# The row maxima of windowed attention, taken off in 16 products of 64 rows instead of 8 of 128

## The reference

```python
def local_attention(q, k, v):              # 8 heads of 64, window of 64 tokens
    ...
    bk, bv = (look_around(bk), look_around(bv))   # each window sees itself and the one before
    sim = jnp.einsum('bhwid,bhwjd->bhwij', bq, bk)
    mask = (i < j) | (i > j + WINDOW) | (j == -1)
    sim = jnp.where(mask, -jnp.finfo(sim.dtype).max, sim)
    attn = jax.nn.softmax(sim, axis=-1)
    out = jnp.einsum('bhwij,bhwjd->bhwid', attn, bv)
```

## Time and profile before

| | us |
|---|---|
| median of 3 runs | 1603.91 |
| the runs | 1602.45, 1603.91, 2719.34 |
| the profiled execution | 1603.7 |
| its span in the trace | 1601.9 |

### The profile page before, as it was taken

The page is one execution under the profiler, slowest core; times in us unless marked ns, Lnnn a source line. Parts: engine busy times, 40 slices in busy tenths (PEclk is TensorE's granted clock), DMA queues, the critical chain, the costliest instruction groups (busy, mean ns, idle before and its releaser), DMA issues.

```text
span 1601.9 us, 46856 instructions
## 1 busy us (share of the span) xinstructions
PE 1433.1 (89%) x19077; PEld 1139.4 (71%) x19077; DVE 1266.0 (79%) x1704; ACT 1288.6 (80%) x1970; POOL 1124.4 (70%) x690
## 2 busy tenths in 40 slices
PE   5999987889999999999997567889999999999998
PEld 3777865677777777777776454777777777777776
DVE  6777757878888888888875867878888888888874
ACT  4876867788888888888886757688888888888885
POOL 3332206778888888888873545778888888888872
PEclk9999999999999999999999879999999999999999
DMA  4312004676666556665650003675666557565662
GB/s 117 103 43 89 20 11 80 129 121 121 114 124 118 115 123 122 118 115 117 119 100 8 1 7 77 128 120 117 120 122 117 117 119 124 123 119 115 117 103 63
DMA packets 359858, 157.50 MB, mean 98 GB/s; under 512 B 299410, under 2 KB 335836, under 8 KB 359644
## 3 DMA queue, kind: packets, MB, share of 16 engines
q1 hardware_dynamic: 359644, 154.51, 48.7%
HBM read 27.29 MB, written 6.29 MB: 21 GB/s over the span
## 4 chain that ended last, share of the span: by engine, by line
PE 36%; ACT 24%; DVE 16%; POOL 9%; issue 8%; DMA 6%; SPq 1%; DVEq 0%; POOLq 0%; ACTq 0%
PE PS L200 6%; PE PS L202 5%; PE PS L201 5%; DMA t<-t 5%; POOL t L1498 5%; POOL t L1504 3%; DVE t L1319 3%; ACT t L1104 3%; ACT t L1125 3%; ACT t L1179 2%; ACT t L1091 2%; PE PS L883 2%; PE PS L902 2%; DVE t L1348 2%; PE PS L858 2%
## 5 line engine op out<-in xcount | busy, mean ns | idle before, releaser
L1498 POOL TENSOR_TENSOR t<-t 128x1024 f32<-128x1024 f32 x128 | 439.7, 3435 | 167.1 <-DVE t L1319 133.7
L1504 POOL TENSOR_TENSOR t<-t 128x512 f32<-128x512 f32 x256 | 320.7, 1274 | 18.4
L1313 DVE TENSOR_REDUCE t<-t 128x16 f32<-128x1024 f32 x128 | 156.0, 1219 | 93.7 <-ACT t L1091 93.7
L200 PE MATMUL PS<-wqh,HH 128*128 128x512 f32 x384 | 170.4, 444 | 33.8 <-DVE t L1319 19.8
L1091 ACT ACTIVATE t<-PS 128x1024 f32<-128x1024 f32 x128 | 131.4, 1026 | 62.3 <-PE PS L202 62.3
L1319 DVE SCALAR_TENSOR_TENSOR t<-t,PS 128x1024 f32<-128x1024 f32 x128 | 155.2, 1213 | 20.1 <-ACT t L1098 20.1
L883 PE MATMUL PS<-t 128*64 128x65 f32 x4096 | 147.5, 224 | 24.3 <-DVE t L1382 22.6
L1348 DVE TENSOR_REDUCE t<-PS 128x8 bf16<-128x1024 f32 x128 | 156.1, 1219 | 15.7 <-PE PS L832 15.5
L1104 ACT CAST t<-t 128x1024 bf16<-128x1024 f32 x128 | 133.2, 1041 | 36.5 <-POOL t L1504 34.3
L1329 DVE TENSOR_TENSOR t<-t 128x1024 f32<-128x1024 f32 x128 | 156.9, 1226 | 4.4
L1336 DVE TENSOR_TENSOR t<-t,PS 128x1024 bf16<-128x1024 f32 x128 | 155.4, 1214 | 6.2 <-ACT PS L1111 6.2
(11 more groups left out here) (252 smaller groups left out, 3597.1 us busy)
## 6 DMA issues: line engine op xcount, KB each, us to landing
t<-t SPq DMA_DIRECT2D x254, 130.0 KB, 2.4
t<-turns SPq DMA_DIRECT2D x128, 128.0 KB, 2.6
t<-yT SPq DMA_DIRECT2D x108, 128.0 KB
t<-t SPq DMA_TRANSPOSE x304, 3.2
t<-in_c_rope SPq DMA_DIRECT2D x32, 128.0 KB, 2.1
turns<-t SPq DMA_DIRECT2D x32, 128.0 KB, 1.9
t<-in_L_attn_a_x SPq DMA_DIRECT2D x4, 512.0 KB, 7.0
t<-yT SPq DMA_DIRECT2D x16, 127.8 KB
```

What stands on the lines that cost most here:

```text
L200: e.matmul(o, ah, bh, start=not more, stop=False, skip_group_check=True)
L1498: e.e.tensor_tensor(BL.tc.rearrange("p (x h) d -> p x h d", x=2), BL.qn.rearrange("p (x h) d -> p x h d", x=2), sin.to_broadcast([128, 2, ...
L1504: e.e.tensor_tensor(tv[:, :, 32 * s:32 * s + 32], tv[:, :, 32 * s:32 * s + 32], BL.tc[:, :, 32 * (1 - s):32 * (1 - s) + 32], ALU.add).then ...
```

## The change

The eight products of L865 become sixteen of half the rows and half the columns, in the order pair, window, parity: an even head's product reads the maxima and the identity from partitions 0 to 63, an odd head's from 64 to 127. The maxima of window w lie in `rows[w]`, so those of the even heads' second window and the odd heads' first window are in the wrong half. DVE therefore copies 64 by 4 numbers down and 64 by 4 up into columns 8 to 11 of a wider `mx`, behind a wait for its own reduction, and PE waits for the two copies (`la_mo`).

```diff
-                           L=arena(sc, [2, 4, RQ * 128 + 64], BF16), mx=[arena(sc, [8], BF16) for _ in range(2)],
+                           L=arena(sc, [2, 4, RQ * 128 + 64], BF16), mx=[arena(sc, [12], BF16) for _ in range(2)],
...
             def take_off_maxima(i):
-                e.wait_ge(S.la_mr, hi(i) + 1)
-                for s in range(2):
-                    for c in range(4):
-                        mm = e.e.matmul(PS[:, 4 + s, 128 * c:128 * c + 128],
-                                        BL.mx[i % 2][:, 4 * s + c:4 * s + c + 1].to_broadcast([128, 128]), idb[:, :],
-                                        start=False, stop=True, skip_group_check=True)
+
+
+                e.wait_ge(S.la_mo, 2 * hi(i) + 2)
+                for c in range(4):
+                    for w in range(2):
+                        for s in range(2):
+                            at, x = 128 * c + 64 * w, (4 * s if w == s else 8) + c
+                            mm = e.e.matmul(PS[:, 4 + s, at:at + 64], BL.mx[i % 2][rows[s], x:x + 1].to_broadcast([64, 128]),
+                                            idb[rows[s], 64 * s:64 * s + 64], start=False, stop=True, skip_group_check=True)
                 mm.then_inc(S.la_s, 1)
...
-                e.e.tensor_reduce(BL.mx[i % 2], PS[:, 2:4, :].rearrange("p s (c k) -> p (s c) k", k=128), AX.X, ALU.max,
+                mx = BL.mx[i % 2]
+                e.e.tensor_reduce(mx[:, 0:8], PS[:, 2:4, :].rearrange("p s (c k) -> p (s c) k", k=128), AX.X, ALU.max,
                                   negate=True).then_inc(S.la_mr, 1)
+                e.wait_ge(S.la_mr, hi(i) + 1)
+                e.e.tensor_copy(mx[0:64, 8:12], mx[64:128, 0:4]).then_inc(S.la_mo, 1)
+                e.e.tensor_copy(mx[64:128, 8:12], mx[0:64, 4:8]).then_inc(S.la_mo, 1)
```

More of the change, by code:

```diff
@@ L64, in build @@
             "tb_ld tr_ld tr_sc tr_st ys_l sl_hi sl_lo ys_f sf_hi sf_lo "
-            "la_pj la_sq la_ss la_rn la_qn la_ta la_tc la_rp la_hi la_hp la_lo la_ht la_lt la_mx la_mr "
+            "la_pj la_sq la_ss la_rn la_qn la_ta la_tc la_rp la_hi la_hp la_lo la_ht la_lt la_mx la_mr la_mo "
             "la_v la_va la_own la_past la_s la_e la_d la_rc la_ot la_ox la_oe la_po la_out la_k0 "
```

## The result

The changed kernel takes 1739.72 us (median of four runs, 1736.05 to 1742.06), before 1605.28 us in the same comparison (median of four). That is 134 us slower, where I had forecast 18. One of the four runs of before took 2719.34 us; the ratio leaves it out and is 1.083, with a 95% interval from 1.080 to 1.085.

The account below looks back on a forecast made before the run. The chain that ended last, not one engine, was taken to bound the kernel. DVE's 31 x 0.43 = 13.3 us and PE's 4.4 us, about +18, on 1603.7 gave 1622 us; the 8-in-10 range was 1600 to 1633.

Parts of the forecast that it names:

- What bounds the kernel: Layers: no engine alone, but the chain that ended last, crossing the engines in turn, 36.6 us per round of four steps.
- What the products cost: PE, L865 to L891: sixteen products take 0.27 us instead of 0.46, a gain of 0.20 us a tile.
- 44 crossings: Times L865 stands on the chain that ended last, so a PE gain counts at most 44 times, not 128.
- What the copies cost: DVE, between reduction and divide: each copy bounded between 0.066 and 0.19 us, taken as 0.155.
- The first rival: DVE's copies are nearly free and PE's gain goes through: below 1608 us, chance 0.18, half of it below 1600.
- The second rival: DVE's copies cost over twice a plain one, 0.28 us each: slower by over 2%, chance 0.10.
- The wait for the reduction, and no overlap: DVE: waiting for its own reduction costs 0.115 us, and each copy its full 0.155 us without overlap.
- D: Delay of DVE's divide by the wait and the two copies: between 0.25 and 0.50 us, taken as 0.43.
- Who waits for DVE: PE's L891 waits for the divide, moving +0.28 or +0.10 us; the products' wait for the copies is hidden.
- The sum: Over the chain's crossings: DVE 13.3 us and PE 4.4 us, together +18 us; for larger D, 60 D - 8.
- the four spare times: How much later the divide could end in each step before PE's transposes wait; predicted examples 0.15, 0.33 and 0.82 us.
- The rivals on the transfers and the clock: Round settles on other transfer waits, 1612 to 1632 us, chance 0.10; PE's lower load lowers its clock, 1668, chance 0.02.

Follow-up runs that it names:

- The products alone: Changed kernel without DVE's wait and two copies, PE waiting for the reduction only, half the products taking another maximum: 1597.04 us, 0.9938 times before.
- four reductions: Changed kernel with two reductions in place of the copies and two more, unread, in front of them: 1653.75 us, 1.0301 times before.

## Why the prediction was wrong

**What bounds the kernel: right.** The chain through DVE's reduction and divide and PE's transposes was the place to look. The loss went through it: in the chain that ended last of the changed kernel L1352 stands 104 times in 128 tiles.

**What the products cost: right.** A gain of 0.20 us a tile was taken, 0.22 was measured at the start of the transposes and 0.17 behind them. That the products themselves took 0.34 up to L894 and not 0.27 doesn't count against it: the 0.80 us of L858 had held the change from 64 to 128 rows, which has only moved. The products alone gave -10 us, the sum with 44 crossings had -7.6.

**What the copies cost: this is the step that failed.** "The two copies are bounded from both sides" by L1307 and L1735, 0.066 to 0.19 us. Both rows are of instructions that read PSUM, and neither of them ran against GpSimd for a way into SBUF. Measured were 0.60 and 0.71 us on average, up to 1.31: I took the shortest price that such a copy can have for its upper end. The trace of before had the rows that show it, outside the two windows that I read, in the self attention ahead of them: a copy of 128 by 128 inside SBUF (L557) and an addition of 128 by 1 with both inputs in SBUF (L548), each seen 32 times (shortest, median and longest in ns), and one of the long ones of L548 in the timeline:

```profile
L557 DVE CAST t<-t x32: 226/228/1249, 48.0 to 225.6; 128x128 fp32r<-128x128 f32 x32
L548 DVE TENSOR_TENSOR t<-t x32: 147/153/1256, 47.3 to 224.9; 128x1 f32<-128x1 f32 x32
...
50.69 1.42 POOL L573 TENSOR_TENSOR t<-t,qks 128x256 f32<-128x256 f32 x1 [2.14 <-DMA t<-in_c_rope]
51.43 0.70 DVE L548 TENSOR_TENSOR t<-t 128x1 f32<-128x1 f32 x1
```

Eleven of the 32 additions of L548 started while GpSimd was at work. They last 0.67 to 1.26 us instead of 0.15, and each ends 0.014 to 0.018 us after the GpSimd instruction. Of the copies of L557 two did, and last 0.65 and 1.25 us instead of 0.23. With these rows and GpSimd busy for 83% of the layers, a copy of up to 1.3 us would have been within the bounds before any experiment.

The first rival's "smallest thing DVE does here" was wrong for the same reason: how many numbers it moves doesn't matter when it waits for another engine. The second rival had the right outcome, slower by over 2%, with 0.10, and its sign, L869 idle for `la_mo`, was seen in 90 tiles; but it had no reason for a dear copy and put the price at 0.28 us each.

**The wait for the reduction, and no overlap: right, but for a gap of 0.03 behind each.** With reductions instead of copies D was 0.49, against 0.43 taken and 0.50 as the upper end.

**Who waits for DVE: right in kind.** L894 waits for the divide in 122 tiles. "This wait is hidden with 0.18 to spare" was right for instructions of 0.155 us (with reductions PE hardly waits for them) and wrong for these: 75.4 us.

**The sum: right for the D it was made for.** D = 0.49 gives 21 us by it, and the kernel with reductions was 21 us slower than before, 1628 where I had forecast 1622. The path fits as well: the sum's 60 D are 31 crossings of the reduction and 29 of the transposes held up by the divide, and L1352 stands 62 times on that kernel's chain. (Counted again, the chain of before has L865 46 times and L1348 followed by L1355 32 times, not 44 and 31; this moves the sum by less than 1 us.) For the D that came it doesn't hold, nor did I say where it ends. In the changed kernel the delays of the divide in the four steps of a round are 1.63, 2.04, 1.70 and 0.52 us, 5.9 together. Less the four spare times, 1.19, this makes 4.7 us a round, and 4.5 without the last step; the round has gone from 36.6 to 41.2 us, 4.5 more. So three of the four steps pay by themselves, each its delay less its spare time. The chain over one round crosses DVE three times (L1352, the copies, L1365, L894 each time), where the earlier trace rows has one crossing; its last row begins the next round:

```profile
540.38 1.14 DVE t L1352
...
544.47 0.66 PE PS L894 x4
...
550.14 1.24 DVE t L1352
...
553.95 0.66 PE PS L894 x4
...
571.07 1.23 DVE t L1352
...
574.82 0.66 PE PS L894 x4
...
581.54 1.15 DVE t L1352
```

The fourth step, with the short copies, isn't on it: from 557 to 567 the chain goes by ACT. The rivals on the transfers and the clock played no part that the trace shows: transfers are 2% of the chain and were 6%, and the granted clock is 0.971 over the whole span, and was 0.973.

## What to carry to other kernels

Before DVE is given a small instruction inside SBUF, look what GpSimd does at that place: a copy, or anything with two inputs in SBUF, can last as long as GpSimd's instruction, here 1.3 us instead of 0.16, while a reduction over an axis of one element did the same work in 0.15. Bound the price of an operation that the trace lacks by rows with the same kind of operands in the same company, not by the smallest ones, and look for them in the whole trace: here they stood in another stage of the program. And a gain on one engine is worth nothing where the next instruction waits for the engine that pays for it.

## What the runs showed of the hardware

- DVE's 64 by 4 copy inside SBUF lasts 0.16 us alone and up to 1.31 us beside GpSimd; all 163 of the longer ones end 0.02 to 0.03 us after a GpSimd instruction does. GpSimd's own busy time is the same as before, 1124.2 us against 1124.4.
- A DVE `tensor_tensor` with two inputs in SBUF does the same (up to 1.29 us), a `tensor_reduce` with one doesn't (0.149 to 0.154 us). In the trace of before an addition of 128 by 1 with two inputs in SBUF already shows it (0.15 us, beside GpSimd 0.67 to 1.26).
- Two independent small DVE instructions on different halves of the partitions start 0.16 to 0.19 us apart (560.40 and 560.56, 560.56 and 560.75 with four reductions), their duration and a gap; for additions on the same partitions, which read PSUM, 0.066 us were seen.
- From the start of PE's last product of 64 rows to the start of the first instruction of 128 rows it takes 0.12 us, before and after the change; sixteen products of 64 rows start within 0.21 us. Four transposes between two such changes took 0.58 us up to the next instruction, behind products of 128 rows 0.44.
